# Graph network and attention: both halves of a step's projection in a row, then the value products and the transposes of all four heads

## The reference, cut to what matters

```python
# layer 0, for each graph b
support = x @ expert_w[top1];  out = adj @ support
y = relu(batchnorm_per_expert(out))
x = layernorm(x + y)                         # x1
# layer 1, for each graph b and head h
q, k, v = split_heads(x @ Wq.T), split_heads(x @ Wk.T), split_heads(x @ Wv.T)
a = (q @ k.T) * D ** (-0.5) + (adj + adj)
p = softmax(a)                               # rows that are all zero give zero
o = p @ v
x = layernorm(x + merge_heads(o) @ Wo.T)
```

## Time and profile before

| | us |
|---|---|
| median of 3 runs (2225.25 to 2225.51) | 2225.41 |
| the profiled execution | 2224.26 |
| its span, first to last instruction | 2222.5 |
| TensorE busy | 2125.2 |
| VectorE busy | 1580.2 |
| ScalarE busy | 1570.8 |
| GpSimd busy | 301.8 |

### The profile page before, as it was taken

The page is one execution under the profiler, slowest core; times in us unless marked ns, Lnnn a source line. Parts: engine busy times, 40 slices in busy tenths (PEclk is TensorE's granted clock), DMA queues, the critical chain, the costliest instruction groups (busy, mean ns, idle before and its releaser), DMA issues.

```text
span 2222.5 us, 42446 instructions
## 1 busy us (share of the span) xinstructions
PE 2125.2 (96%) x14627; PEld 1683.8 (76%) x14627; DVE 1580.2 (71%) x4012; ACT 1570.8 (71%) x3509; POOL 301.8 (14%) x659
## 2 busy tenths in 40 slices
PE   6999999589999999999999999999999999999996
PEld 5778887467777777777777777777777777777774
DVE  5887877366767676767676768686868686868675
ACT  3544443187878787878787878787878787878785
POOL 0000000110202020202020202020202020202011
PEclk9999999799999999999999999999999999999999
DMA  6444342677777777777777777777778777777761
GB/s 237 160 155 148 133 150 94 130 119 127 141 129 139 128 140 128 140 126 142 134 133 133 134 133 135 132 136 132 134 130 138 134 135 131 136 135 133 131 100 45
DMA packets 149008, 297.18 MB, mean 134 GB/s; under 512 B 14514, under 2 KB 14546, under 8 KB 148690
## 3 DMA queue, kind: packets, MB, share of 16 engines
q1 hardware_dynamic: 137490, 256.97, 61.8%
q0 software_dynamic: 11328, 37.76, 6.0%
HBM read 110.12 MB, written 50.33 MB: 72 GB/s over the span
## 4 chain that ended last, share of the span: by engine, by line
PE 71%; issue 13%; ACT 8%; DVE 6%; DMA 1%; POOL 0%; SPq 0%; DVEq 0%; ACTq 0%; POOLq 0%
PE bank L605 28%; PE bank L651 17%; PE bank L635 11%; PE bank L620 8%; ACT prob L872 3%; DVE prob L1166 2%; PE bank L525 2%; ACT probT L770 2%; PE bank L542 2%; PE bank L577 1%; PE bank L643 1%; DVE z L1130 1%; DVE st_ln L1123 1%; DMA qp<-stage_q 1%; ACT v L844 1%
## 5 line engine op out<-in xcount | busy, mean ns | idle before, releaser
L1166 DVE CUSTOM_DVE_ANT_0 prob<-bank,adj_sb 128x512 f32<-128x512 f32 x1024 | 657.7, 686 | 140.8 <-PE bank L620 140.8
L872 ACT ACTIVATE prob<-prob,neg_max 128x512 f32<-128x512 f32 x1024 | 731.3, 723 | 9.4 <-DVE neg_max L1175 5.4
L770 ACT ACTIVATE probT<-bank 128x512 f32<-128x512 f32 x832 | 460.3, 594 | 320.4 <-PE bank L651 318.0
L651 PEld LDWEIGHTS bank<-ident,prob 128*128 128x128 f32 x4096 | 463.6, 140 | 111.9 <-issue 51.9
L651 PE MATMUL bank<-ident,prob 128*128 128x128 f32 x4096 | 541.1, 275 | 5.6 <-ACT probT L770 4.3
L620 PE MATMUL bank<-kp,qp 128*128 128x512 f32 x1024 | 348.5, 422 | 31.1 <-DVE row_max L1166 21.6
L1180 DVE COPY probT<-bank 128x512 f32<-128x512 f32 x192 | 131.6, 686 | 235.9 <-PE bank L651 235.9
L635 PE MATMUL bank<-probT,v 128*32 128x256 f32 x4096 | 247.6, 382 | 0.8 <-issue 0.8
L620 PEld LDWEIGHTS bank<-kp,qp 128*128 128x128 f32 x1024 | 176.4, 190 | 64.5 <-DVE row_max L1166 34.4
L872 ACT ACTIVATION_READ_ACCUMULATOR prob<-prob,neg_max 128x1 f32 x1024 | 204.4, 200 | 0.0
L605 PE MATMUL bank<-xT,wkT 128*128 128x512 f32 x768 | 202.3, 399 | 0.0
(11 more groups left out here) (112 smaller groups left out, 2088.7 us busy)
## 6 DMA issues: line engine op xcount, KB each, us to landing
kp<-stage_k SPq DMA_DIRECT2D x256, 256.0 KB, 6.7
qp<-stage_q SPq DMA_DIRECT2D x256, 256.0 KB, 8.5
x_raw<-in_x_dram SPq DMA_DIRECT2D x16, 1024.0 KB, 7.5
adj_raw<-in_adj_t_dram SPq DMA_DIRECT2D x16, 1024.0 KB, 9.7
outT_spill<-outT SPq DMA_DIRECT2D x16, 1024.0 KB, 5.1
v<-outT_spill SPq DMA_DIRECT2D x16, 1024.0 KB, 15.1
z<-in_x_dram POOLq DMA_DIRECT2D x64, 256.0 KB, 3.1
adj_sb<-in_adj_dram SPq DMA_DIRECT2D x64, 256.0 KB, 8.1
```

The costliest lines, as they stand in the source:

```text
L651: ins = nc.tensor.transpose(t_bank[j % 2][:, mt * P:(mt + 1) * P], prob[:, s % 2, j, mt * P:(mt + 1) * P], ident[:, :])
L770: return nc.scalar.activation(dst, src, ACT.Copy, scale=scale)
L872: nc.scalar.activation(prob[:, s % 2, j, :], prob[:, s % 2, j, :], ACT.Exp, scale=2.0, bias=neg_max[:, s % 2, j:j + 1], accum_out=row_sum[ ...
L1166: nc.vector.tensor_tensor_reduce(prob[:, s % 2, j, :], s_bank[j][:, :], adj_sb[:, t, :], 1.0, LOWEST, ALU.add, ALU.max, row_max[:, g % 2, ...
```

## The change

TensorE issues the second half of the projection directly behind the scores of head 3, ahead of the value products and of the transposes of heads 0 and 1. Before, it stood between the transposes of head 1 (and `y_rows` or `x1_transpose`, where a step has them) and those of head 2. The order of everything else, and what the late steps 8 and 9 do, stays.

```diff
                     next_scores((3,))
+                    if not late:
+                        dense_half(1)
                     if s > 0 and s % 2 == 0:
                         weigh_v(b, s - 1, par)
                     elif s == 0 and not first:
...
                         pe.wait_ge(*reader[other])
                         x1_transpose(b + 1, XT_MIDDLE[s], dense_bank[other])
                         reader[other] = (xT_lo, NT * (b + 1) + XT_MIDDLE[s] + 1)
-                    if not late:
-                        dense_half(1)
-
                     if last and s == STEPS - 2:
```

## The result

The changed kernel takes 2310.53 us (median of 4 runs, 2308.84 to 2311.82) against 2225.46 us (4 runs, 2225.25 to 2226.25): ratio 1.0383, 95% interval 1.0368 to 1.0397. It is slower by 85 us; 89 were forecast. The profiled execution took 2308.84 us, 84.6 more than the one of before.

A forecast was written before the change was run, and what follows sets the result against it. TensorE, busy 96% of the span, was taken as the bound. Fourteen middle batches at 5.68 us (79.5), the first 5.3 and the last 4.4 add 89.2 us to 2224.3: 2313.5, or 2314; range 2285 to 2345, 84%.

The forecast's parts named there:

- Plain short steps: Steps 1, 3, 11, 13, 15: uncovered copies of two transpose banks stop TensorE for 0.50 and 0.10 us, +0.60 each.
- rival B: TensorE changes its kind of work less often, so seams repay 0.1 us at two places per projection: 2271 us, 5%.
- Plain long steps: Steps 0, 2, 12, 14, which also hold value products: the same pauses less seam differences, +0.49 us each.
- The seam that no row showed: Second half to value products in long steps: taken as 1.45 us, between bounds of 1.36 and 1.54.
- Steps 4 and 5: Step 5's y_rows already wait for ScalarE's relu of step 4, so both steps together lose only 0.12 us.
- Steps 6 to 9: Other transposes cover the copy in part and VectorE's idle 0.93 us goes: together about 0.45 us lost.
- the 1.00 us wait in step 8: Scores of head 3 wait for VectorE there; the wait was to become shorter or vanish.
- Step 10: Four x1 transposes stay between the two pairs and cover the copy: +0.15 us.
- step 11: Counted as a plain short step, with its copies uncovered: +0.60 us.
- step (5) of the prediction: ScalarE keeps up: its heaviest round takes 5.94 us, against at least 6.07 between two steps' first transposes.
- Rival A: ScalarE falls behind, every short step pays 0.59 us more, 62 us in all: 2376 us, 5%.
- Rivals C and D: C, 4%: the copy is not waited for, 2209 us; D, 2%: pauses lower TensorE's clock, 105 us more, 2420.

The follow-up runs named there:

- e6: The kernel before with the second half moved ahead in step 5 alone: 2219.89 us, ratio 0.9975.
- e1: The changed kernel with only three of the second half's six matmuls moved ahead, three left between the transpose pairs: 2234.1 us, ratio 1.0038.
- e11: e1 with step 12 left as in the kernel before, all six matmuls in the gap: 2238.27 us, ratio 1.0064.

## Why the prediction was right

The time, the mechanism and most terms held. Point by point, the terms for one middle batch:

- Plain short steps: +0.60 forecast, +0.48 to +0.54 measured in steps 1, 3, 13 and 15. The two pauses came as taken from the earlier trace rows (1.28 and 0.90 us). The term that was too high is the second half in front of the transposes: 1.46 us in the sum, 1.38 measured (1264.36 to 1265.74). The 0.08 belongs to the first matmul behind transposes, and the second half no longer follows any; I had put it at the other end of the six. This is a piece of rival B.
- Plain long steps: +0.49 forecast, +0.50 to +0.52 measured in steps 0, 2 and 12, +0.43 in step 14. The seam that no row showed, second half to value products, is 1.45 us (1270.29 to 1271.74), the value taken.
- Steps 4 and 5: +0.12 forecast, +0.05. The parts are +0.52 in step 4, which is a plain long step, and -0.47 in step 5; e6 shows the second by itself: with the second half ahead, TensorE no longer waits for the relu.
- Steps 6 to 9: +0.45 forecast, +0.53, of which 0.42 in step 8. That the 1.00 us wait in step 8 would shrink was wrong: it is 1.03. VectorE is ahead as forecast (the scores of head 3 start 11.43 us after the first transposes of step 6, 12.27 before), but TensorE reaches them sooner by as much, since one half of a projection less stands behind those transposes. The prediction left that out of its account of the wait. The sum was right because I took it from VectorE's chain, not from the wait.
- Step 10: +0.15 forecast, +0.05; step 11: +0.60 forecast, +0.73, as the projection of k waits for the last split of x1. That wait was not in the sum.
- ScalarE keeps up, as in step (5) of the prediction: from 556 to 2235 us the longest idle time that the trace shows for the copies is 0.3 us (147 times, 36.9 us in all), where a late ScalarE shows 0.79. Rival A did not happen.
- Rivals C and D: the pause is open in every plain step, and the clock is 1.00. The rule of the Trainium skill ("TensorE: Matmul & The Clock Gate", section "Loop structure matters more than you think"), whose own example of a cold loop is a long wait for a DMA ahead of every matmul, did not bite: waits of 0.5 us for another engine left the clock at 1.00.

The sum for a middle batch was 5.68 us and is 5.38; fourteen make 4.2 of the 4.6 us by which the forecast of the added time (89.2) is above the 84.6 of the two profiled executions. Part of this closeness is luck: the plain short steps, steps 4 and 5 and step 10 came out 0.5 us a batch below the sum, steps 6 to 9 and step 11 0.2 above it.

## What to carry to other kernels

Where two PSUM banks alternate between TensorE and a copying engine, other work should stand between the two uses of a bank. Here three matmuls in the gap (0.68 us) hid the pause as well as six, and one (0.23) left half of it. The rest could go elsewhere without a pause, though not for nothing: in e1 step 14 paid 0.57 us through a late transfer. Before moving work, look for a place in the same trace where that work is missing; the steps without a projection gave the two distances to 0.01 us. The move costs 0.5 us in a step where the projection was the only cover, and gains 0.5 in step 5, where TensorE waited for the relu and y_rows cover the copy. So such an order is worth choosing step by step.

## What the runs showed of the hardware

- The first 512-column matmul behind 128-column transposes took about 0.08 us more than the others: six matmuls take 1.38 us up to the next transposes when they follow scores, 1.46 when they follow transposes (1240.05 to 1241.51 in the earlier trace rows).
- The idle time that the trace gives TensorE in such a pause is half of what the starts show (0.25 against 0.50 us).
- The transfers of q within SBUF, four of 256 KB each, took up to 8.8 us from issue to landing in the kernel before and up to 9.3 and 9.4 in e1 and e11, in the batch that the rows show. On average over 14 batches the last one landed 0.80 us later in e11, issued at the same time. The k transfers ahead of it had been issued 0.68 later; that these are the cause is likely and not shown.
